# Third attention: dense queries in place of queries kept once per head with zeros

## What is computed

```
q = (x @ Wq).reshape(B, N, 4, 32)     # k likewise, v and g with width 64
gk = log_sigmoid(x @ Wgk + bgk) / 16  # one gate per token and head
A[t, s] = (q[t] . k[s]) * 32 ** -0.5 * exp(G[t] - G[s])   for s <= t, G = cumsum(gk)
o = A @ v
o = o * rsqrt(mean(o * o) + eps) * gnorm_w * silu(g)
out = o @ Wo
```

## Time and profile before

| | |
|---|---|
| median of 3 runs | 1882.08 us (1879.52 to 1883.31) |
| profiled execution | 1879.0 us, its span 1877.2 us |
| mean granted TensorE clock | 0.951 of full speed |
| busy, TensorE products | 1677.5 us (89% of the span) |
| busy, VectorE | 1485.5 us (79%) |
| busy, ScalarE | 1262.7 us (67%) |
| busy, GpSimd | 463.4 us (25%) |

### The profile page before, as it was taken

One profiled execution on the slowest core, in us unless ns is written; L12 is line 12 of the kernel. 1 busy time (PEld: TensorE's weight loads), 2 busy tenths in 40 slices (PEclk: granted clock), 3 DMA queues, 4 the chain that ended last, 5 costly groups with the idle time before them and its releaser, 6 DMA issues. The chain is left out here.

```text
span 1877.2 us, 45866 instructions
## 1 busy us (share of the span) xinstructions
PE 1677.5 (89%) x16705; PEld 1046.0 (56%) x16710; DVE 1485.5 (79%) x3615; ACT 1262.7 (67%) x3357; POOL 463.4 (25%) x596
## 2 busy tenths in 40 slices
PE   6999988969779999957689999999959999998786
PEld 6999963447634444446444444444436666566454
DVE  4444468968689999878789999999958887788575
ACT  5666647856646655577578888888855666656675
POOL 2000001328401111110212222222213444336233
PEclk9999989979879999979789999999969999999899
DMA  3200006300034444100266666666500000000000
GB/s 89 87 4 4 4 13 252 141 1 2 14 124 165 164 163 161 75 1 2 74 227 226 229 226 228 229 230 228 211 23 24 23 1 23 24 1 1 1 11 16
DMA packets 52464, 174.80 MB, mean 93 GB/s; under 512 B 7376, under 2 KB 32976, under 8 KB 34896
## 3 DMA queue, kind: packets, MB, share of 16 engines
q1 hardware_dynamic: 52304, 172.59, 25.5%
HBM read 168.05 MB, written 2.95 MB: 91 GB/s over the span
## 5 line engine op out<-in xcount | busy, mean ns | idle before, releaser
L950 DVE TENSOR_TENSOR ps<-ps,m_comb 128x512 f32<-128x512 f32 x520 | 363.3, 699 | 22.3 <-DMA m_comb<-m_shares 6.7
L935 DVE TENSOR_TENSOR m_hwlo<-ps,m_hwhi 128x512 f16<-128x512 f32 x520 | 353.9, 681 | 0.3
L910 ACT ACTIVATE m_hwhi<-ps 128x512 f16<-128x512 f32 x520 | 308.2, 593 | 21.3 <-DVE ps L950 19.9
L916 ACT ACTIVATE ps<-ps 128x512 f32<-128x512 f32 x388 | 225.8, 582 | 81.1 <-PE ps L865 81.0
L865 PE MATMUL ps<-x_hi,m_whi 128*128 128x512 f16 x652 | 249.4, 383 | 8.8 <-DVE m_hwlo L935 5.8
L865 PE MATMUL ps<-x_lo,m_whi 128*128 128x512 f16 x652 | 249.2, 382 | 0.0
L865 PE MATMUL ps<-x_hi,m_wlo 128*128 128x512 f16 x652 | 249.1, 382 | 0.0
L836 POOL CAST m_whi<-m_stage 128x256 f16<-128x256 f32 (+1 forms) x130 | 55.0, 423 | 629.7 <-PE ps L871 617.5
L485 DVE TENSOR_TENSOR rn_s_lo<-ps,rn_s_hi 128x32 f16<-128x32 f32 x512 | 98.2, 192 | 132.8 <-ACT ps L449 132.8
L871 PE MATMUL ps<-m_hwhi,m_whi 128*128 128x512 f16 x520 | 197.6, 380 | 0.3 <-DVE m_hwlo L935 0.2
L871 PE MATMUL ps<-m_hwlo,m_whi 128*128 128x512 f16 x520 | 197.4, 380 | 0.0
(11 more groups left out here) (478 smaller groups left out, 3969.7 us busy)
## 6 DMA issues: line engine op xcount, KB each, us to landing
m_comb<-m_shares SPq DMA_DIRECT2D x128, 1024.0 KB, 5.1
m_stage<-in_m_w SPq DMA_DIRECT2D x97, 128.0 KB, 4.5
m_stage<-in_m_w SPq DMA_DIRECT2D x33, 192.0 KB, 4.7
kept_lj_w<-in_lj_w SPq DMA_DIRECT2D x6, 1024.0 KB, 4.9
kept_lq_w<-in_lq_w SPq DMA_DIRECT2D x1, 1600.0 KB, 8.1
kept_la_w<-in_la_w SPq DMA_DIRECT2D x1, 1280.0 KB, 6.7
rn_rows<-in_L_attn_rows SPq DMA_DIRECT2D x4, 256.0 KB, 3.8
rn_xs<-rn_xn_hi SPq DMA_DIRECT2D x32, 32.0 KB, 1.9
```

What stands on the lines that cost most here:

```text
L910: nc.scalar.activation(hw_hi[:, k % HB, :], weighted(k), ACT.Copy).then_inc(hi_done, 1)
L916: nc.scalar.activation(acted(k), ps[:, 4, :] if gated else bank(k), func).then_inc(act_done, 1)
L935: nc.vector.tensor_tensor(hw_lo[:, k % HB, :], weighted(k), hw_hi[:, k % HB, :], ALU.subtract)\
L950: nc.vector.tensor_tensor(weighted(k), bank(k), comb[:, s, n * QW:(n + 1) * QW], ALU.mult)\
```

## The change

The query tiles have one copy, [128, 2048], with the rows of all four heads. ScalarE and VectorE split each quarter of the queries with one instruction over 128 rows in place of four over 32. The two fills with zeros and the wait for them go. The score products take the 32 rows of their head from keys and queries, and no longer all 128.

```diff
-        q_hi = sb("lg_qhi", [P, H, N], F16)
-        q_lo = sb("lg_qlo", [P, H, N], F16)
+        q_hi = sb("lg_qhi", [P, N], F16)
+        q_lo = sb("lg_qlo", [P, N], F16)
...
-                nc.gpsimd.memset(q_hi[:].rearrange("p h n -> p (h n)").bitcast(F32), 0.0).then_inc(zero_s, 1)
-                nc.gpsimd.memset(q_lo[:].rearrange("p h n -> p (h n)").bitcast(F32), 0.0).then_inc(zero_s, 1)
...
-                    for h in range(H):
-                        r = slice(h * DK, (h + 1) * DK)
-                        nc.scalar.activation(q_hi[r, h, cut], ps[r, n, :], ACT.Copy)
+                    nc.scalar.activation(q_hi[:, cut], ps[:, n, :], ACT.Copy)
...
-                act.wait_ge(zero_s, 2)
...
-                act.wait_ge(zero_s, 3)
+                act.wait_ge(zero_s, 1)
...
-                    for h in range(H):
-                        r = slice(h * DK, (h + 1) * DK)
-                        nc.vector.tensor_tensor(q_lo[r, h, cut], ps[r, n, :], q_hi[r, h, cut], ALU.subtract)
+                    nc.vector.tensor_tensor(q_lo[:, cut], ps[:, n, :], q_hi[:, cut], ALU.subtract)
...
+                        r = slice(h * DK, (h + 1) * DK)
                         for a in range(TB):
-                            lhs = [t[:, bass.ds(seq * T + a * P, P)] for t in (k_hi, k_lo)]
-                            rhs = [t[:, h, bass.ds(seq * T + a * P, T - a * P)] for t in (q_hi, q_lo)]
+                            lhs = [t[r, bass.ds(seq * T + a * P, P)] for t in (k_hi, k_lo)]
+                            rhs = [t[r, bass.ds(seq * T + a * P, T - a * P)] for t in (q_hi, q_lo)]
```

## The result

The changed kernel takes 1884.8 us (median of 20 runs, 1879.7 to 1895.9), the kernel before 1880.5 (20 runs beside them, 1878.7 to 1883.3): ratio 1.0027, 95% interval 1.0017 to 1.0038. It is slower by some 5 us, where 9.25 us less were forecast. The profiled execution took 1885.5 us (span 1883.7; before 1877.2). The changed kernel's times spread more than those of the kernel before, and its longest run (1895.9 us) has the lowest mean clock of the twenty, 0.867, against 0.878 in the profiled one. (A run's mean clock comes near 0.88 or near 0.95 for any of the kernels, without a difference in time: from 100 to 200 us e1's trace shows a clock of 0.50 with 2922 products, that of the kernel before 1.00 with 2921. So the record is not to be trusted there, and only means near one another are compared. In the loop the durations of the products bear it out.)

A forecast was written before the change was run, and what follows sets the result against it. Query and key splitting on ScalarE and VectorE was taken to bound the stretch before the third attention's loop, VectorE the loop's pace. Splits -9.7 and loop head +0.45 gave -9.25 us: 1882.1 to 1872.8, range 1869.5 to 1878.

The forecast's parts named there:

- Splits: Ahead of the third attention's loop: fewer query copies and subtractions let the subtraction of gates start 9.7 us earlier.
- about 3: Sign in the changed profile: TensorE's wait in front of the gate rows is about 3 us, from 11.0.
- what is late next: At the join ahead of the loop: ScalarE's copy of the gate rows becomes the late one, by 0.2 us.
- rival A: Ahead of and at the loop's head: shorter idle keeps the clock at 2.4 GHz, 1.3 us more gain, 1871.5; chance 0.08.
- Memsets and layout: Removing two GpSimd fills of 3.5 us and shrinking the query tiles by four was held to gain nothing.
- A border and a plain step: In the loop: each tile-size change costs 0.10 us, 0.10 to 0.20 at half clock; TensorE needs 1.25 a plain step.
- I count nothing for them: Borders in the loop's plain steps: lag of 0.3 to 0.4 us fits the room, so 0; other end 6.4 us.
- From the third step VectorE sets the pace again: In the loop: only its head loses time, +0.45 us; then VectorE's 1.155 us a step rules.
- Rival D: In the loop: clock falls as 32-row products take a third of TensorE's time; +16 less 9.7, 1888; chance 0.02.
- the last stage's 0.99: Argument against a falling loop clock: the stage with most of the 32-row products runs at granted clock 0.99.
- rival B: In the loop: borders show on the path, fully exposed 6.4 us and 1878.8, half of it 1875.6; chance 0.12.
- Rival C: In the loop: same-row-group loads are exposed, a plain step takes 1.85 us, total +4, 1886; chance 0.04.

The follow-up runs named there:

- e1: Changed kernel with score products over all 128 rows of the dense queries and keys, no borders: ratio 0.9947 to the kernel before.
- e13: Changed kernel with 20 useless 128-row, 512-column products in TensorE's two pauses ahead of the loop: ratio 0.9981 to the kernel before.
- e5: Changed kernel with four extra 128-column products on 128 rows ahead of each head's scores: ratio 1.0055 to the kernel before.
- e6: Changed kernel with four extra 128-column products on 32 rows ahead of each head's scores: ratio 1.0066 to the kernel before.
- e9: Changed kernel with score products on rows 0 to 65 of dense queries and keys, no borders: ratio 0.9959 to the kernel before.
- e12: Changed kernel with 66-row score products and a 32-row, 8-column product ahead of each head's scores, two borders a step: ratio 0.9994 to the kernel before.
- e10: Kernel before with a 32-row, 8-column product ahead of each of a head's two score groups, four borders a step: ratio 1.0030.
- e3: Kernel before with one extra 32-row, 8-column product ahead of each head's 128-row scores, two borders a step: ratio 1.0020.
- e11: Changed kernel's dense splits, SyncE transfers into padded tiles (quarters 1 to 3 in the second block), scores on 128 rows: ratio 0.9939 to the kernel before.

## Why the prediction was wrong

*Splits.* Right in mechanism, a little small: 9.7 us forecast for the splits, 10.4 seen. TensorE's wait is 2.73 us ("about 3"), and what is late next is ScalarE's copy of the gate rows, as said. From TensorE's 832.27 to 833.33 it took 1.06 us, where I had 1.31, since the gate-row products ran at full clock (0.29 us); that is the small piece of rival A that came. e1 shows the whole gain in the time (some 10 us).

*Memsets and layout.* Nothing was forecast for them, and e1's 10 us leave nothing to assign.

*A border and a plain step.* 0.10 us at full clock, 0.10 to 0.20 at half: 0.09 and 0.13 to 0.14. A plain step 1.25 us: 1.24.

*The step that failed* is "I count nothing for them" (the borders in the plain steps), with "From the third step VectorE sets the pace again": +0.45 us was forecast for the loop, and the second block got 14.8 us longer, at 2.19 us a plain step where VectorE's 1.155 was to set the pace. Both take for granted that the loop gets to full clock as before, within some 5 us. Before, TensorE had pauses in it and yet was at 0.97; the changed loop was busy without a pause, at half clock, for its first 36 us. Rival D ("the clock falls in the loop, since a third of TensorE's time is spent on a quarter of the rows") is what came, with its price: half-clock step 2.2 us forecast, 2.19 seen; +16 forecast, +14.8 in the profile. I gave it 0.02. That its figures fit so well is in part luck: the 2.2 had one border of 0.10 where two of 0.13 to 0.14 came, so the rest of the step was put too high, and the +16 took all 32 steps at half clock, where 54 of 68 us were.

The reason against D was the last stage's 0.99. That row was read wrongly. It shows that few rows can go with full clock, in a stage that is at full clock already and where TensorE is busy 25.4 of 30 us. It doesn't show that a loop that starts at half clock rises on such products. The earlier trace rows had the other half of the warning: 0.50 in the first steps. e13 shows what this start is worth: 6 to 8 us of the block. The rest is a fall inside the loop, in a pause of 1.34 us, from which the clock was back after 20.4 us.

D's own reason was incomplete too. Few rows are a part of it (128 to 66 without borders: clock 0.95 to 0.83; in the profiles also e5 against e6). Borders are as large a part of the time: 6.6 us between e9 and e12. They lengthen each step in a loop that has 0.1 us of room (rival B, 6.4 us if fully exposed), but that the two figures are alike doesn't show that the 6.6 are such time, as the clock may have a share in them. Alone they leave a full clock at full in e10's profile; e3's longer runs had a lower mean clock, so I can't rule out that they cost clock by themselves.

The Trainium skill ("TensorE: Matmul & The Clock Gate", Part 1) says that idleness throttles TensorE and being busy releases it. The falls agree with it, as each lies in a pause or close behind one. For the release the trace disagrees with these products: 36.1 of 36.1 us busy at the lower level. The measurement decides.

*Rival C*, the loads of one row group, did not come: the 256-column products of one head follow each other after 0.11 to 0.12 us at full clock on the same 32 rows, and a step of 1.24 leaves no room for it.

**What stays open.** What exactly the clock follows: neither rows nor borders nor the start alone give it, and why some pauses bring a fall and others as long don't isn't shown. No run takes the pauses out of a 32-row loop that starts at full clock, which would test whether they are what makes it fall. The seven runs of e3 that were 5 to 10 us longer than its profiled one had a lower mean clock, but where in the program isn't located; nor are the 2 us of e10 outside the block.

## What to carry to other kernels

Cutting a product's rows saved TensorE no time here and cost it the clock: where a loop's TensorE work at full clock is near the bound (here 1.05 of 1.155 us a step), work out the step at half clock too, and ask at which clock the loop starts and what could lift it. A clock seen in another stage speaks only for a stage with the same start, pauses and products. And the gain of a change can often be kept apart from its cost: here dense copies stay, and hidden transfers restore the form that the products had.

## What the hardware showed unexpectedly

- A loop on 32-row products between 128-row ones stayed at half clock for its first 36 us with TensorE busy throughout; with full clock at its start it held it for 18 us and then fell, in a pause of 1.34 us.
- It rose again right after eight transposes or six 512-column products on 128 rows (at 871.8 and 899.2; in e13 at 874.3).
- The first rise came 3.4 to 5.9 us into a loop of 128-row products and 36.8 to 56.1 us into one with 32-row products.
- Changing between tile sizes costs 0.09 us at full clock and 0.13 to 0.14 at half, for 32 and for 64 rows; 66 rows cost no border (0.11 us to the next product at half clock).
- Twenty useless products in two pauses of together 4.8 us made a kernel 4 to 5 thousandths faster.
- 24 of e11's 32 transfers of 32 KB from SBUF to SBUF, issued mostly every 0.63 us and landed after 1.9 in the median, ran beside the loop at no cost that shows.
